# A two-layer graph network: half a component of the first layer's outer product as sixteen scaled copies on ScalarE, and the turn of the product ahead of the scalar sums

## What is computed

```python
agg = segment_sum(messages(x[col], edge_attr), row)      # edges into nodes
a0, a1 = split(agg); x0, x1 = split(x)                   # 64 scalars, 32 x 3 vectors
u0 = einsum('eu,ev,uvw->ew', x0, y0, wu000) \
   + INV_SQRT3 * einsum('euk,evk,uvw->ew', x1, y1, wu110)   # y0 = a0, y1 = a1
u1 = einsum('eu,evk,uvw->ewk', x0, y1, wu011) + einsum('euk,ev,uvw->ewk', x1, y0, wu101)
x  = layernorm(2*x + merge(u0 + x0 @ lu0, u1 + x1 @ lu1))
```

## Time and profile before

| | us |
|---|---|
| time, median of 3 runs | 6489.07 (6481.88 to 6490.79) |
| the profiled execution's own time | 6484.03 |
| its span, first to last instruction | 6482.3 |
| VectorE busy | 5447.3 (84%) |
| TensorE busy | 5231.3 (81%) |
| GpSimd busy | 5135.4 (79%) |
| ScalarE busy | 3699.9 (57%) |

### The profile page before, as it was taken

The page is one execution under the profiler, slowest core; times in us unless marked ns, Lnnn a source line. Parts: engine busy times, 40 slices in busy tenths (PEclk is TensorE's granted clock), DMA queues, the critical chain, the costliest instruction groups (busy, mean ns, idle before and its releaser), DMA issues.

```text
span 6482.3 us, 133337 instructions
## 1 busy us (share of the span) xinstructions
PE 5231.3 (81%) x45695; PEld 4209.8 (65%) x45695; DVE 5447.3 (84%) x7293; ACT 3699.9 (57%) x11728; POOL 5135.4 (79%) x4006
## 2 busy tenths in 40 slices
PE   5667666666666489999999999999938888888888
PEld 3445555555555367777777777777737777777776
DVE  6777777777777489999999999998919999999999
ACT  2333333333333266666666666666628888888887
POOL 2777777777777558888888888887869999889998
PEclk7787788888887699999999999999969999999999
DMA  7888888888887358888888888888748888888886
GB/s 228 253 263 260 257 257 261 260 257 253 260 258 228 113 167 270 278 274 276 275 274 276 273 279 270 274 269 267 243 143 232 235 236 231 229 230 233 234 234 191
DMA packets 752721, 1588.26 MB, mean 245 GB/s; under 512 B 126847, under 2 KB 508461, under 8 KB 725935
## 3 DMA queue, kind: packets, MB, share of 16 engines
q1 hardware_dynamic: 599311, 1298.29, 66.5%
q0 software_dynamic: 152736, 281.45, 12.8%
HBM read 792.00 MB, written 787.28 MB: 244 GB/s over the span
## 4 chain that ended last, share of the span: by engine, by line
PE 34%; ACT 17%; DMA 14%; POOL 12%; issue 9%; DVE 7%; SPq 6%; POOLq 0%; ACTq 0%; DVEq 0%
POOL slots L694 8%; PE node_ps L1435 7%; ACT onehot L1790 7%; DMA slots<-pay,slot_all 6%; PE prods_ps L1362 5%; PE s_ps L1276 3%; PE node_ps L1391 3%; POOL q L777 3%; DMA xt<-x_mid 3%; PE prods_ps L1379 3%; PE m_ps L1276 2%; DMA rec<-edge_recs 2%; ACT win L1790 2%; POOL q L812 2%; PE prods_ps L1403 2%
## 5 line engine op out<-in xcount | busy, mean ns | idle before, releaser
L694 POOL DMA_INDIRECT slots<-pay,slot_all x3136 | 3246.5, 1035 | 1037.9 <-issue 815.1
L1276 PE MATMUL m_ps<-win,picks_sb 125*128 125x160 f32 x3136 | 668.2, 341 | 432.1 <-ACT pay L1587 426.0
L1146 DVE TENSOR_REDUCE upd<-work 125x48 f32<-125x3072 f32 x300 | 1004.0, 3347 | 6.9
L1133 DVE TENSOR_TENSOR work<-prods_ps,yv 125x1024 f32<-125x1024 f32 x800 | 930.4, 1214 | 52.1 <-PE prods_ps L1366 50.2
L1276 PEld LDWEIGHTS m_ps<-win,picks_sb 125*128 125x128 f32 x3136 | 526.9, 217 | 521.2 <-issue 419.7
L1790 ACT ACTIVATE onehot<-node_iota,msgs 128x125 f32<-128x125 f32 x2550 | 783.0, 392 | 122.2 <-POOLq L738 122.2
L1435 PEld LDWEIGHTS node_ps<-msgs,onehot 128*125 128x125 f32 x5100 | 701.7, 189 | 101.3 <-ACT onehot L1796 40.1
L1435 PE MATMUL node_ps<-msgs,onehot 128*125 128x160 f32 x5100 | 738.2, 303 | 35.9 <-ACT onehot L1796 14.2
L777 POOL TENSOR_TENSOR q<-xt,yv 125x3072 f32<-125x3072 f32 x100 | 548.0, 5480 | 133.7 <-PE turn_ps L1422 116.2
L1572 ACT COPY picks_sb<-s_ps 125x512 f32<-125x512 f32 x392 | 229.8, 586 | 553.8 <-PE s_ps L1258 497.2
L812 POOL TENSOR_TENSOR q<-q 125x1024 f32<-125x1024 f32 x200 | 473.9, 2370 | 15.7
(11 more groups left out here) (290 smaller groups left out, 14005.8 us busy)
## 6 DMA issues: line engine op xcount, KB each, us to landing
msgs<-slots SPq DMA_DIRECT2D x200, 1428.0 KB, 10.4
slots<-zero SPq DMA_DIRECT2D x183, 1386.0 KB
win<-table SPq DMA_DIRECT2D x784, 160.0 KB, 2.7
zs<-x_t SPq DMA_DIRECT2D x500, 250.0 KB, 5.4
picks<-picks_sb SPq DMA_DIRECT2D x196, 512.0 KB, 11.7
picks_sb<-picks SPq DMA_DIRECT2D x196, 512.0 KB
table<-tab SPq DMA_DIRECT2D x200, 350.0 KB
slots<-pay,slot_all POOLq DMA_INDIRECT x3136
```

The lines of the kernel that those rows point to most:

```text
L694: g.indirect_dma_start(out=slots[layer][:, :], out_offset=bass.IndirectOffsetOnAxis(ap=slot_all[:, j:j + 1], axis=0), in_=pay[q][:, j - UB ...
L1133: ve.tensor_tensor(wk[:, i, :, :].rearrange("p w (h k) -> p h w k", h=2), prods_ps[((nb if layer == 0 else 0) + r) % 2][0:HM, :].rearrange ...
L1146: ve.tensor_reduce(upd1[:, :, w0:w0 + ROUND // KV], mixed_part(r), AX_X, ALU.add).then_inc(s["upd"], 1)
L1276: mm = te.matmul(to[:, D * j:D * j + D], (pick_b[q] if layer else pick_n[hh])[0:WROWS, P * (2 * p + j):P * (2 * p + j) + P], win[q][0:WROW ...
```

## The change

VectorE (and GpSimd in the first seven tiles) no longer makes the second half of part 2 of `q3`. ScalarE makes it, as sixteen copies of 32 columns: each copies the 32 summed components of a node and scales them by one of the node's own 16 components as a per-partition scale. They stand in three groups: five between `paid(0,0)` and `paid(0,1)`, five between `paid(0,1)` and the distances, six between `paid(0,2)` and the selections. A new semaphore `q_scaled` counts them, and the addition of part 2 waits for it. A tile has 3 `q_part` in place of 4. VectorE's `q_first` and `q_add` are changed as `outer_rest` in the diff. On TensorE `turn_q(0)` moves ahead of `scalar_sums`, and `message(1,0)` moves from between the two turns to behind `turn_y`; on ScalarE `paid(1,0)` moves ahead of `scalars_out`.

```diff
-Q_PARTS = (4, 2)
+Q_PARTS = (3, 2)
...
             def outer_rest(k):
-                for i, u0 in ((0, 0), (2, V // 2)):
-                    g.tensor_tensor(*q_factors(nb, i, u0), ALU.mult).then_inc(s["q_part"], 1)
+                g.tensor_tensor(*q_factors(nb, 0, 0), ALU.mult).then_inc(s["q_part"], 1)
                 for i in (1, 2):
                     g.wait_ge(s["q_mul"], Q_MULS[0] * n + i + 1)
-                    g.wait_ge(s["q_part"], Q_PARTS[0] * n + 1 + i)
+                    g.wait_ge(s["q_part"], Q_PARTS[0] * n + i)
+                    if i == 2:
+                        g.wait_ge(s["q_scaled"], n + 1)
...
                 sum_edges()
+                turn_q(0)
                 scalar_sums()
-                turn_q(0)
-                message(1, 0)
                 turn_q(1)
                 turn_y()
+                message(1, 0)
                 vector_products()
...
+                def scaled_rows(u0, u1):
+                    if not nodes:
+                        return
+                    if u0 == V // 2 and within(n, 1, NT):
+                        ac.wait_ge(s["q_part"], Q_PARTS[0] * n)
+                    for u in range(u0, u1):
+                        last = ac.activation(q3[0:HM, 2 * VV + V * u:2 * VV + V * u + V], yv[nb][0:HM, 2, 0:V], ACT.Copy,
+                                             scale=xt[nb][0:HM, S + 3 * u + 2:S + 3 * u + 3])
+                    if u1 == V:
+                        last.then_inc(s["q_scaled"], 1)
...
                 paid(0, 0)
+                scaled_rows(V // 2, V // 2 + 5)
                 paid(0, 1)
+                scaled_rows(V // 2 + 5, V // 2 + 10)
                 if edges:
                     distances(0, k, HOT[2], HOT[3])
                 normal()
                 paid(0, 2)
+                scaled_rows(V // 2 + 10, V)
                 if edges:
                     selections(0, 3 * t + 3, HOT[2], HOT[3]).then_inc(s["hot"], 1)
...
                 turned_y()
+                paid(1, 0)
                 scalars_out()
-                paid(1, 0)
```

More of the change, by code:

```diff
@@ L311, in layer_sems @@
                 s[n] = sem(f"{n}_l{layer}")
-            for n in (("picked", "pick_turned", "pick_out", "out0", "lin_out"), ("copied", "mixed_mul", "x_put", "scaled", "scaled_used", "out0"))[layer]:
+            for n in (("picked", "pick_turned", "pick_out", "out0", "lin_out", "q_scaled"), ("copied", "mixed_mul", "x_put", "scaled", "scaled_used", "out0"))[layer]:
                 s[n] = sem(f"{n}_l{layer}")
@@ L1106, in q_first @@
                         ve.wait_ge(s["q_turned"], 2 * n)
-                    for i, u0 in ((0, 0), (2, V // 2)):
-                        ve.tensor_tensor(*q_factors(nb, i, u0), ALU.mult).then_inc(s["q_part"], 1)
+                    ve.tensor_tensor(*q_factors(nb, 0, 0), ALU.mult).then_inc(s["q_part"], 1)
                 def q_add(i):
@@ L1114, in q_add @@
                     ve.wait_ge(s["q_mul"], Q_MULS[0] * n + i + 1)
-                    ve.wait_ge(s["q_part"], Q_PARTS[0] * n + 1 + i)
+                    ve.wait_ge(s["q_part"], Q_PARTS[0] * n + i)
+                    if i == 2:
+                        ve.wait_ge(s["q_scaled"], n + 1)
                     ve.tensor_tensor(q3[0:HM, 0:VV], q3[0:HM, 0:VV], q3[0:HM, VV * i:VV * i + VV], ALU.add).then_inc(s["q_part"], 1)
```

## The result

| | before | after |
|---|---|---|
| median of the runs, us | 6488.4 (6481.88 to 6490.79) | 6865.64 (6863.24 to 6878.79) |
| ratio to before, 95% interval | 1 | 1.0591 (1.0578 to 1.0604) |
| span of the profiled execution, us | 6482.3 | 6861.6 |

The forecast was 6826, between 6672 and 6900. The kernel is 377 us slower where 338 were forecast.

The account below looks back on a forecast made before the run. The prediction took a TensorE-ScalarE loop through the selections as the bound. Copies +2.94, order -0.98 and clock +1.38 made +3.34 us a step, 339 us with the six earlier steps: 6826 us, range 6672 to 6900.

Parts of the forecast that it names:

- What bounds the kernel: Middle stage: each step is one loop, TensorE from edge sums to messages, then about 4.4 us of ScalarE up to the selections.
- the sum: Middle stage: +2.94 - 0.98 + 1.38 = +3.34 us a step over 94 steps, 25 us for six earlier ones; 6826 us.
- Part 1: VectorE's removed multiplication, 682 ns a step from tile 7 on: gains nothing, as the loop doesn't pass through VectorE.
- Part 2: Sixteen ScalarE copies before the selections: 0.213 us each, 3.41 in all, 0.47 hidden, edge sums 2.94 us later.
- Part 3: New order on TensorE between scalar_sums and vector_products: all 0.98 us a step of waiting for ScalarE's copies of the turned product go.
- Part 4: TensorE stands still about 3.05 us before the edge sums, its clock falls and they run slow: +1.38 us a step.
- the clock stays up: Rival: TensorE's idle stretch before the edge sums leaves its clock alone; 198 us slower, 6687 by the median; chance 0.2.
- Short copies: Rival: ScalarE's copies take 0.086 us each, like plain ones; -0.08 us a step, 6481 to 6489; chance 0.1.
- long copies: Rival: ScalarE's copies are as long as the distances, 4.67 us for sixteen; about 6980; chance 0.1 together with a no-gain order.

Follow-up runs that it names:

- the split sums: The order alone, and the copies in idle time, each with turn_q(0) placed after the first quarter of scalar_sums: 6429.3 and 6431.8 us.
- the filled stretch: The changed kernel plus eleven unused identity multiplications on TensorE between message(0,3) and the edge sums in each step: 6663.9 us, ratio 1.0281.

## Why the prediction was right, and which term was off

*What bounds the kernel*: right. The loop of TensorE and ScalarE through the selections set the step; the idle 4.1 us of ScalarE in front of `summed` were no cover where the copies were put and became one where they were moved behind `paid(0,3)`. One reading was too short: ScalarE's idle time in before is not one stretch, since the earlier trace rows have 80.5 us in 40 steps more, 2.0 a step, in front of the copies of the turned product. Nothing in the sum hangs on it.

*Part 1, VectorE's 0.68 us are worth nothing*: right, shown twice: the order alone and the copies in idle time differ by less than 20 us, and with the split sums not at all. The wait in front of `h` grew, as said. One sign failed: VectorE's busy time was to be lower by some 0.6 us a step and is 22.4 in before and after, because the multiplication that it kept took 0.5 us longer in the changed kernel (last section). With the copies in the idle time it is lower, 21.9, and still nothing is gained.

*Part 2, the copies*: right, nearly to the digit. 0.213 us each were forecast from the distances with their per-partition bias, 0.212 measured; the stretch for which TensorE stands still was to be 3.05 us and is 3.04. The Trainium skill, "ScalarE: Activation LUTs", section "What ACT_TABLE_LOAD costs", gives 186 ns and 0.833 ns a column for an instruction, 93 more for a per-partition operand, and 93 less where one follows another, from which an estimate of 213 ns for 32 columns follows; the trace agrees. The Trainium skill's factor of three ("ScalarE: Activation LUTs", section "Rules for kernel authors"), which it states per element and for bf16, doesn't give the time of these short fp32 copies: an estimated 2.05 us by it, 3.4 measured.

*Part 3, the order*: right. 0.98 us were forecast, 1.06 came (5.14 to 4.08) in the changed kernel, where VectorE's addition is in time. By itself the order is worth less, since there the addition is late.

*Part 4, the clock*: the mechanism was right, and its size is what was off. I took 1.38 us a step from 26 stretches of the first stage, of which 5 did nothing. In the changed kernel each of the 94 stretches in steps with messages brought the clock down, and the edge sums lost 6.81 - 4.72 = 2.09 us. Two things made the difference. The first is how often it falls. Length is a part of that: the stretches here are 3.0 us long, those of the first stage were mostly shorter, and with 2.4 us in this very step half of them do nothing. But it isn't all of it. The five that did nothing in the first stage weren't its shortest, the last of the earlier trace rows with 2.92 us among them; and in the changed kernel itself one of 3.15 us, in a step before messages begin and 2 us after an earlier fall had ended, left the clock at 1.00 (the stretch, and 5 us behind it):

```profile
2331.08:2334.23 3.15, 0.00 (x1) 0.00 (x1) 3.12 (x4) 3.15 (x12) 0.70 (x1) 1.00 0.15 38
2334.23:2339.23 5.00, 5.00 (x37) 5.00 (x38) 4.53 (x3) 0.58 (x3) 1.66 (x1) 1.00 0.01 2
```

What else decides it stays open. The second is what a fall costs: the edge sums lose 1.4 to 1.7 us where the clock stays down for 3.4 us, and 2.7 to 3.0 where it stays down for 6.8; the 5 us windows of the earlier trace rows can't show more than 2.5. With 2.09 in place of 1.38 and 1.06 in place of 0.98 the sum, from a step in the middle of the stage before, is 24.72 + 2.94 - 1.06 + 2.09 = 28.69 a step against 28.67 measured. The clock's term alone makes 0.71 x 94 = 67 us more than forecast, 6893 by the median, close to the upper end of the range. That the kernel came in at 6866 was not foreseen: the order's 0.08 us more a step give back some 8 us, and the last steps of the stage some 7, as in before they were 25.2 us long, not 24.72, led by a wait for a transfer that the trace after doesn't have. The rest was not followed up.

*The rivals*: "the clock stays up" is what the filled stretch built, and it costs 6664 where 6687 was its price. Short copies and long copies are out by the measured 0.212 us. (The price of the short copies has a slip: 8 us less than 6484 is 6476, and the 6481 given for it is already the figure by the median.)

## What to carry to other kernels

An engine's idle time covers new work only if the work is put into it, behind what the other engines wait for: in the same new order, the kernel with sixteen copies of 3.4 us ahead of the selections takes 6866 us and with the same copies behind them 6459, on the same engine in the same step. Before a step is moved to an engine that is idle for a third of the time, follow the chain of waits through that engine and see on which side of its wait the new work falls. And when the bound is TensorE, price the time for which it will stand still twice: for itself, and for what its clock does to the matmuls behind, which in these steps was 2.1 us on average for a stretch of 3.0, a third of that for 2.4 and nothing for 1.7.

## What the runs showed of the hardware that I had not expected

After one and the same idle stretch of 3.04 us the lower clock lasted 3.4 us in one step and 6.8 in another, with the same work behind it. Nor is it chance which: from 2676 us to the end of the stage the steps last 28.26, 27.98, 29.32, 28.26 and 29.54 us and then the same five again, in this order.

VectorE's one remaining multiplication for the product got slower when the other one was taken away. Groups by shape, 3200 to 4200 us, before, after, and in the kernel with the copies in idle time:

```profile
L1108 DVE TENSOR_TENSOR q<-xt,yv 125x1024 f32<-125x1024 f32 x40 | 48.5, 1213 | 0.0
```
```profile
L1108 DVE TENSOR_TENSOR q<-xt,yv 125x1024 f32<-125x1024 f32 x35 | 60.2, 1721 | 0.0
```
```profile
L1108 DVE TENSOR_TENSOR q<-xt,yv 125x1024 f32<-125x1024 f32 x41 | 49.8, 1215 | 0.0
```

In the changed kernel it meets a multiplication of GpSimd's, as at 3525 us (VectorE's, then GpSimd's, in order of time):

```profile
3525.30 1.52 DVE L1108 TENSOR_TENSOR q<-xt,yv 125x1024 f32<-125x1024 f32 x1
```
```profile
3524.66 1.07 POOL L751 TENSOR_TENSOR q<-xt,yv 125x512 f32<-125x512 f32 x1
3525.90 1.81 POOL L694 DMA_INDIRECT slots<-pay,slot_all  x1 [0.17 <-issue]
```

VectorE's ends at 3526.82, 1.09 us after GpSimd's has ended, so it is as if it had started only about then; and GpSimd's next DMA takes 1.81 us, where most take 0.96, and ends 0.9 us after VectorE's. The Trainium skill, "SBUF — State Buffer", section "SBUF: two separate sides", says that VectorE with two SBUF operands and GpSimd take turns at a shared port for whole instructions; the trace agrees. It costs nothing that a run here shows: VectorE waits 5.3 us a step in front of `h` afterwards.
